# Order of units, key statistics and bias steps in the last stretch of a two-layer transformer kernel

## The reference, cut to what matters

```python
k = _layernorm(k, kn_g, kn_b)
v = _layernorm(v, vn_g, vn_b)
kv = jnp.einsum('bhqd,bhqe->bhde', k, v) / Q * temperature + attn_bias
att = jnp.einsum('bhqd,bhde->bhqe', q, kv)
...
h = jax.nn.gelu(att @ p1_w.T + p1_b, approximate=False)
return h @ p2_w.T + p2_b + x
...
scores = jax.nn.softmax(xf @ w_router, axis=-1)
expert_weights, top_experts = jax.lax.top_k(scores, TOP_K)
order = jnp.argsort(flat_e, stable=True)
...
valid = offsets < capacity
slot = jnp.where(valid, bin_ids * capacity + offsets, E * capacity)
xb = jnp.zeros((E * capacity + 1, hs), x.dtype).at[slot].set(xf[src])
h = jax.nn.gelu(jnp.einsum('ech,ehf->ecf', xb, w1))
y = jnp.einsum('ecf,efh->ech', h, w2).reshape(E * capacity, hs)
out = jnp.zeros((T, hs), x.dtype).at[src].add(flat_w[order][:, None] * yv)
return out.reshape(sl, bs, hs) + bias
```

## Time and profile before

| | us |
|---|---|
| median of 3 runs | 976.9 |
| lowest, highest | 976.89, 980.12 |
| the profiled execution | 977.13 |
| its span (first to last instruction) | 975.3 |
| TensorE, VectorE, ScalarE, GpSimd busy | 909.6, 705.4, 636.0, 370.7 |

### The profile page before, as it was taken

One profiled execution on the slowest core, in us unless ns is written; L12 is line 12 of the kernel. 1 busy time (PEld: TensorE's weight loads), 2 busy tenths in 40 slices (PEclk: granted clock), 3 DMA queues, 4 the chain that ended last, 5 costly groups with the idle time before them and its releaser, 6 DMA issues.

```text
span 975.3 us, 17867 instructions
## 1 busy us (share of the span) xinstructions
PE 909.6 (93%) x6484; PEld 650.3 (67%) x6484; DVE 705.4 (72%) x1857; ACT 636.0 (65%) x1097; POOL 370.7 (38%) x444
## 2 busy tenths in 40 slices
PE   5597988998999999999999999999999997999996
PEld 3354644554667878777777777777777565999972
DVE  8988886777769786686877878687786758763324
ACT  4477768777797677667677777776776565554420
POOL 4346053124001001242645427164552423178881
PEclk9698988999999999999999999999999998999998
DMA  5844344346123245310111111111112322122416
GB/s 130 232 132 124 74 109 122 103 111 216 60 69 67 64 110 111 67 43 24 65 44 47 41 50 38 44 66 44 42 47 94 102 71 81 28 64 82 119 40 235
DMA packets 86180, 83.15 MB, mean 85 GB/s; under 512 B 8979, under 2 KB 72457, under 8 KB 86093
## 3 DMA queue, kind: packets, MB, share of 16 engines
q1 hardware_dynamic: 80868, 73.33, 26.8%
q0 software_dynamic: 4320, 8.27, 2.5%
q10 hardware_dynamic: 904, 0.42, 0.1%
HBM read 50.54 MB, written 31.72 MB: 84 GB/s over the span
## 4 chain that ended last, share of the span: by engine, by line
PE 72%; DVE 18%; ACT 4%; issue 3%; POOL 1%; DMA 1%; POOLq 0%; SPq 0%; DVEq 0%; ACTq 0%
PE psum L1560 18%; PE psum L1602 10%; PE psum L1597 6%; PE psum L1583 5%; PE psum L1396 5%; PE psum L1334 3%; DVE pieces L2097 3%; DVE maxes L1976 2%; PE psum L1377 2%; PE psum L1350 2%; PE psum L1410 2%; PE psum L1517 1%; PE psum L1474 1%; PE psum L1495 1%; PE psum L1304 1%
## 5 line engine op out<-in xcount | busy, mean ns | idle before, releaser
L1560 PE MATMUL psum<-parts,q_stack 128*128 128x512 f32 x640 | 251.7, 474 | 6.8 <-DVE parts L2294 5.7
L2587 ACT ACTIVATE big<-psum,cols 128x512 f32<-128x512 f32 x205 | 139.7, 687 | 80.3 <-PE psum L1560 76.3
L2811 POOL TENSOR_TENSOR hT<-hT,gb_tok 128x512 f32<-128x512 f32 x54 | 77.2, 1430 | 268.7 <-DVE gb_tok L2112 267.9
L1560 PEld LDWEIGHTS psum<-parts,q_stack 128*128 128x128 f32 x640 | 113.0, 191 | 59.9 <-issue 40.9
L1560 PE MATMUL psum<-parts,k_stack 128*128 128x512 f32 x320 | 126.8, 396 | 0.0
L1976 DVE TENSOR_REDUCE maxes<-psum 128x4 f32<-128x1024 f32 (+1 forms) x96 | 114.0, 1214 | 16.5 <-PE psum L1350 16.1
L1602 PE MATMUL psum<-big,ew 128*128 128x512 f32 x234 | 119.4, 594 | 0.0
L1597 PE MATMUL psum<-pieces,w_parts 128*128 128x512 f32 x336 | 97.9, 399 | 0.0
L2891 POOL DMA_INDIRECT routed<-big,slot_i x64 | 66.0, 1032 | 50.7 <-DVE slot_i L2281 29.1
L2097 DVE TENSOR_TENSOR pieces<-big,pieces 128x512 fp32r<-128x512 f32 x88 | 74.1, 847 | 11.4 <-ACT pieces L2594 11.3
L2914 POOL DMA_INDIRECT answers<-hT,to x64 | 62.7, 980 | 43.7 <-DVE hT L2309 27.3
(11 more groups left out here) (432 smaller groups left out, 1945.4 us busy)
## 6 DMA issues: line engine op xcount, KB each, us to landing
gb_tok<-gate_rows SPq DMA_DIRECT2D x32, 512.0 KB, 3.6
q_stack<-q_pieces SPq DMA_DIRECT2D x32, 192.0 KB, 3.6
k_stack<-k_pieces SPq DMA_DIRECT2D x32, 192.0 KB, 4.6
routed<-empty_row SPq DMA_DIRECT2D x4, 1040.0 KB, 8.6
big<-routed SPq DMA_DIRECT2D x16, 260.0 KB, 3.0
answers<-empty_row SPq DMA_DIRECT2D x4, 1024.0 KB, 7.7
q_pieces<-gb_tok SPq DMA_DIRECT2D x16, 192.0 KB, 2.1
k_pieces<-gb_tok SPq DMA_DIRECT2D x15, 192.0 KB, 2.1
```

Source lines behind the costliest of these rows:

```text
L1560: last = eng.matmul(bank(i), w1_part(wp, e)[:, fs], parts[2 * xk + xp][:, :], start=n == 0, stop=n == 2)
L2587: eng.activation(slots[held("slot", "up", n, e, f)], bank(held("bank", "up", n, e, f)), ACT.Relu, bias=col("L0_ffn_b1", e * FC + f)).then_ ...
L2811: eng.tensor_tensor(hT[:, ns], xpT[:, ns] if e == 0 else hT[:, ns], gate_wide[:, e // GHELD % 2, e % GHELD, :], ALU.add).then_inc(sem("acc ...
```

## The change

Five edits in `order_steps`; no emitting function is changed.

```diff
-        p.step("la_r", n, work="dve:3.4", after=[("la_s", b) for b in batches], rank=rank, chain=(20 + n, BPC * n, 2),
+        p.step("la_r", n, work="dve:3.4", after=[("la_s", b) for b in batches] + ([("ft", u) for u in range(2)] if n == NCH - 1 else []), rank=rank, chain=(20 + n, BPC * n, 2),
...
-        p.step("ft", u, work="pe:.45 act:.6 dve:.69", urgent=8 if u < 2 else 0, after=[("fetch", u)], rank=at - 150, opens=[(0, split), (0, bank)],
+        p.step("ft", u, work="pe:.45 act:.6 dve:.69", urgent=40 if u < 2 else 0, after=[("fetch", u)], rank=at - 150, opens=[(0, split), (0, bank)],
...
-            p.step("up2", u, f, work=f"pe:.77 act:{1.9 if u < 2 and f == 0 else .64}", after=[("ft", u), ("sw", 1, e)] + ([(("up2", u, f - 1), "pe")] if f else []), rank=at + f,
+            p.step("up2", u, f, work=f"pe:.77 act:{1.9 if u < 2 and f == 0 else .64}", after=[("ft", u), ("sw", 1, e)] + ([(("up2", u, f - 1), "pe")] if f else [(("up2", 0, FC - 1), "pe")] if u == 1 else []), rank=at + f,
...
-        p.step("ans", u, work="dve:1.75", after=[("down2", u, CT - 1), *[("rt_b", b) for b in range(RINGS * CHUNK // S)]]
+        p.step("ans", u, work="dve:1.75", urgent=6 if u < EARLY else 0, after=[("down2", u, CT - 1), *[("rt_b", b) for b in range(RINGS * CHUNK // S)]]
...
-        p.step("bias", b, work="dve:1.1", urgent=-40, after=[("sg_m", 1, k) for k in range(B // 4)] + [("ln_z", 1, 1, b)], chain=(92, b, 0),
+        p.step("bias", b, work="dve:1.1", urgent=-40, after=[("sg_m", 1, k) for k in range(B // 4)] + [("ln_z", 1, 1, b), ("ans", (7 + b // 2))], chain=(92, b, 0),
```

## The result

The changed kernel takes **970.33 us** (median of 5 runs, 968.45 to 972.24), the kernel before beside it 978.05 us (5 runs). The ratio is 0.9911 with a 95% interval of 0.9896 to 0.9925: 0.9% faster, and inside the range of the prediction. The profiled execution took 968.45 us, its span 966.7.

What follows compares the result with a forecast made beforehand. The prediction took the last chunk's slots (`rt_w 7`) plus a fixed GpSimd stretch as the bound. Terms of 2.6, 4.2 and 0.6 us, minus 0.6 for bias steps, plus 0.2 tail, gave 7.0 us: 969.9 us from 976.9, range 967.9 to 973.4.

Steps and rivals of the forecast that it cites:

- The bound: At the end: the last chunk's slots (`rt_w 7`) plus a fixed GpSimd stretch of scatters and sends set the end.
- First term: Up to L1675 on TensorE, with splits ahead of `la_r`: L1675 starts at 829.0, before 831.59, 2.6 us earlier.
- ends at 827.0: VectorE's key statistics `la_r` start at 821.8 and end at 827.0, 1.8 us later than before.
- Second term: L1675 to L1750 on TensorE: fewer unit steps and no standing still, 24.2 us in place of 28.45, 4.2 us gained.
- Third term: From L1750 to the slots: VectorE now waits, L2263 comes 0.45 us after L1750, before 1.04; 0.6 us gained.
- Bias steps beside issues: Bias steps behind answers 7 to 14 stretch GpSimd's gapless issuing: minus 0.6 us, bounds 0 and 1.9.
- Rival C: GpSimd issues held up by every bias operation for its whole length, 18.0 us lost: 987.3 us, slower; chance 0.05.
- Tail: After the last send: TensorE's gap before the last sums falls to 3.6 us; 0.2 us gained.
- the second case of the prediction: In the tail: the clock stays up, and VectorE's last sums bound the gain at 1.1 us.
- Sum: Whole kernel: 7.4 - 0.6 + 0.2 = 7.0 us gained.
- B: Rival: TensorE's clock falls all the same near 823, matmuls up to L1750 lose about 2.3 us: 972.2 us; chance 0.13.
- D: Rival: waits, not TensorE's queue, bind the route to the slots; little beyond the first term holds: 974.3 us; chance 0.11.

Runs made afterwards that it cites:

- fewer_pauses: The changed kernel with the sends of units 10 to 13 issued without their three GpSimd memsets each: 968.08 us, ratio 0.9879 to the kernel before.
- more_tensor: The changed kernel with 2.8 us more TensorE work ahead of unit 13's first up2 and three filler products fewer: 972.20 us, ratio 0.9916 to the kernel before.
- undo_up2: The changed kernel with unit 1's up2 steps again free to go in turn with unit 0's on TensorE: 968.28 us, ratio 0.9903 to the kernel before.
- undo_bias: The changed kernel with the bias steps back where they were free to stand: 973.54 us, ratio 0.9950 to the kernel before.
- no_pauses: The changed kernel with no memsets at all behind the sends of units 2 to 13: 965.86 us, ratio 0.9855 to the kernel before.
- order_alone: The kernel before with only the edge that puts unit 0's up2 steps ahead of unit 1's: 979.89 us, ratio 0.9997 to the kernel before.
- undo_splits: The changed kernel with the last chunk's key statistics not waiting for the splits, which are as urgent as before: 977.92 us, ratio 0.9986 to the kernel before.
- only_bias: The kernel before with the late bias steps alone: 976.48 us, ratio 0.9973 to the kernel before.

## Why the prediction was right

It was right in time, sign and mechanism. Its terms were mostly too small, which a later start of the stage and a slower kernel beside it made up for.

- **The bound**, `rt_w 7` plus a fixed GpSimd stretch: shown by fewer_pauses (2.55 us off the stretch, 2.53 off the last issue) and borne out by more_tensor. One correction, from undo_up2: the stretch begins with the slots *or* unit 2's answers.
- **First term**, 2.6 us: measured 3.71. The prediction's steps hold up to `la_r`: casts at 819.96 (measured 820.76, less the 0.87 of the start), a hole of 1.1 (0.98), L2148 at 821.8 (821.70 by the same count). Its step "ends at 827.0" failed: it took `la_r`'s 5.20 us over unchanged, though 1.08 of them were L2151 waiting for GpSimd. `la_r` took 4.2 us, and L1675 came 1.1 us sooner than forecast.
- **Second term**, 4.2 us: measured 4.02, L1675 to L1750 24.43 us against 24.2. The size was right and the heading wrong: with the unit order undone this stretch is still 25.69 us, so 1.3 us belong to "unit 0 ahead of unit 1" and 2.8 to the other edits together. That the unit steps in this stretch set its length is borne out by the seven profiles of the table: without them, at the prediction's prices, 7.3 to 8.5 us are left in each.
- **Third term**, 0.6: measured 0.68.
- **Bias steps beside issues**, minus 0.6: measured minus 0.1. Of GpSimd's 64 issues 13 lay beside bias steps; three were stretched, by 0.10 to 0.16 us, and ten took 0.97 or 0.98. Rival C is refuted. The section of the Trainium skill that the prediction cites for it (SBUF — State Buffer, "Who interferes with whom") also says, further on, that a two-input VectorE operation takes the read interface alone and that writing a DMA's descriptors needs the write interface (inferred, it adds). The trace agrees with that, and I should have read it as evidence against C.
- **Tail**, 0.2: measured 1.16, just over the upper bound of 1.1. TensorE idled 2.80 us in place of the 3.6 forecast, since GpSimd came 8.3 us earlier and TensorE's filler 6.8. The clock fell for a shorter time, and the gain still came to what the second case of the prediction allows, the bound by VectorE's last sums (with the reads ahead of them).
- **Sum**, 7.0: 9.47 behind the stage's start in the profiles, less 0.87 for a later start. The medians of the comparison differ by 7.7 us, and the forecast started from 976.9 where the kernel before took 978.05 beside the changed one. That 969.9 lies so near 970.33 is in part luck.
- **B** did not happen (granted clock 1.00 from 822 to 830), nor did **D**: L1304 and L1750 show no idle time before them.

## What to carry to other kernels

Find the engine whose queue has no wait left up to the end, and price a change by how much earlier that stretch begins; here 4.78 us of TensorE's idle time stood in a kernel that was 2.5 us faster, and 2.8 us of extra matmuls cost the last issue 0.6. Before a duration is carried over to a new place in the order, compare it with the same instruction's other instances: 1.37 us against 0.29 was a hold-up by a neighbour that the new order avoided. And once the bound is known, cut it directly: the memsets between the sends were worth another 0.6%, until TensorE became the bound.

## What the runs showed of the hardware

- A VectorE operation on fp32 data in SBUF stood until GpSimd's `tensor_tensor` had ended, for up to 1.08 us: L2151 1.37 us in place of 0.29, L2331 1.46 in place of 0.43, and L2151 as a `tensor_scalar` with one input 1.31. Reductions (L2148), and splits that read PSUM and one SBUF operand (L2294, 1.28 us for two beside a product in undo_bias), ran at their usual speed.
- A VectorE cast of fp32 to int32 in SBUF stood until GpSimd's memsets had ended: L2302 took 1.43 us in place of 0.16 in the changed kernel and 0.78 in undo_bias; in no_pauses, with no GpSimd work beside it, 0.16.
- Indirect DMA issues on GpSimd were not held up in this way: beside bias steps at most 1.13 us in the changed kernel for 0.97. The pitch of 1.28 us between scatters (942.45 to 943.73 and on) is the same in all kernels. Single ones in other runs took 1.40 (undo_bias), 1.42 (order_alone) and 1.43 us (more_tensor), each beside an operation of `sum 0`.
- Ahead of the last sums TensorE's clock stayed at the higher level after idle times of 0.20 to 1.46 us (fewer_pauses, undo_bias, undo_up2, undo_splits, only_bias) and fell after 2.80 to 8.13 us. After 8.13 us it returned sooner than after 4.33 us (18 matmuls in 10.00 and 11.01 us).
